# Attention and FFN block on one core: the second head's weights loaded and bounded in the preamble, the third head's loaded one head sooner

## The reference

```python
def attn(hidden_states, wq, wkv, wo):          # H=32, DN=DV=128, DQ=192
    q = (hidden_states @ wq).reshape(B, S, H, DQ)
    kv = hidden_states @ wkv                   # k: first H*DN columns, v: next H*DV
    scores = einsum('bqhd,bkhd->bhqk', q[..., :DN], k) * DQ ** (-0.5)
    probs = softmax(where(causal, scores, -1e30), axis=-1)
    attn = einsum('bhqk,bkhd->bqhd', probs, v).reshape(B, S, H * DV)
    return attn @ wo
x = x + attn(layernorm(x), wq, wkv, wo)
x = x + ffn(layernorm(x), k0, s0, k1, s1, k2, s2)
```

## Time and profile before

| | us |
|---|---|
| median of 3 runs (lowest, highest) | 1177.06 (1173.53, 1177.54) |
| the profiled execution's own time | 1173.75 |
| its span | 1171.9 |
| PE busy | 1092.5 (93%) |
| DVE busy | 895.7 (76%) |
| ACT busy | 677.0 (58%) |
| POOL busy | 677.7 (58%) |
| start of head 1's first scores on PE | 91.61 |

### The profile page before, as it was taken

One profiled execution on the slowest core, in us unless ns is written; L12 is line 12 of the kernel. 1 busy time (PEld: TensorE's weight loads), 2 busy tenths in 40 slices (PEclk: granted clock), 3 DMA queues, 4 the chain that ended last, 5 costly groups with the idle time before them and its releaser, 6 DMA issues. The chain is left out here.

```text
span 1171.9 us, 22406 instructions
## 1 busy us (share of the span) xinstructions
PE 1092.5 (93%) x6216; PEld 655.7 (56%) x6216; DVE 895.7 (76%) x1799; ACT 677.0 (58%) x1335; POOL 677.7 (58%) x694
## 2 busy tenths in 40 slices
PE   4658999999999999999999999999999999999898
PEld 3424555656556565656555565656555565655577
DVE  6556778787878787887878787887877787886873
ACT  5446565656566565656566556656566556655453
POOL 2406766656666766656666756656666756655400
PEclk9878999999999999999999999999999999999999
DMA  3126574646554474645554474545654474644601
GB/s 125 28 70 112 99 125 85 126 102 125 98 113 87 98 128 83 123 104 125 101 115 82 101 130 83 122 103 123 107 112 76 102 130 83 117 91 83 118 1 72
DMA packets 367800, 117.41 MB, mean 100 GB/s; under 512 B 313248, under 2 KB 361632, under 8 KB 367776
## 3 DMA queue, kind: packets, MB, share of 16 engines
q1 hardware_dynamic: 367776, 117.12, 50.9%
HBM read 39.45 MB, written 2.12 MB: 35 GB/s over the span
## 5 line engine op out<-in xcount | busy, mean ns | idle before, releaser
L1113 PE MATMUL psC<-xb,wqk 128*128 128x512 f16 x1350 | 323.7, 383 | 6.4 <-ACT x L671 4.1
L978 DVE CUSTOM_DVE_ANT_0 psS<-psS,mask,undo_qk 128x128 f32<-128x128 f32 (+7 forms) x256 | 210.9, 824 | 117.3 <-PE psS L1113 103.7
L549 POOL TENSOR_TENSOR qkT<-qk,qkT 128x512 f16<-128x512 f32 x124 | 143.1, 1159 | 246.5 <-ACT qkT L712 246.5
L1113 PE MATMUL psC<-wos,attn 128*128 128x512 f32 x768 | 249.7, 435 | 28.5 <-DVE attn L968 26.8
L719 ACT ACTIVATE psS<-psS,negmax 128x128 f32<-128x128 f32 (+7 forms) x256 | 182.6, 713 | 136.4 <-DVE negmax L978 134.2
L1113 PE MATMUL psS<-qkT 128*128 128x512 f16 (+3 forms) x1152 | 232.5, 330 | 24.4 <-DVE p L985 12.0
L985 DVE SCALAR_TENSOR_TENSOR p<-psS,p 128x128 f16<-128x128 f32 (+7 forms) x256 | 192.6, 753 | 42.3 <-ACT p L727 40.8
L1113 PEld LDWEIGHTS psC<-xb,wqk 128*128 128x128 f16 x1350 | 123.9, 98 | 162.2 <-issue 34.0
L1231 PE MATMUL psC<-pT,v 128*128 128x512 f16 (+3 forms) x1152 | 199.5, 328 | 0.8 <-DMA pT<-p 0.6
L1001 DVE SCALAR_TENSOR_TENSOR res<-psC,rinv,res 128x512 f32<-128x512 f32 x256 | 189.3, 744 | 6.9 <-DVE rinv L992 3.3
L1113 PE MATMUL psC<-wvs,xb 128*128 128x256 f16 x1536 | 190.5, 275 | 0.0
(11 more groups left out here) (90 smaller groups left out, 925.4 us busy)
## 6 DMA issues: line engine op xcount, KB each, us to landing
raw<-in_L_attn_wkv SPq DMA_DIRECT2D x64, 256.0 KB, 3.5
raw<-in_L_attn_wq SPq DMA_DIRECT2D x32, 256.0 KB, 3.5
raw<-in_L_attn_wo SPq DMA_DIRECT2D x32, 256.0 KB, 4.0
pT<-p SPq DMA_TRANSPOSE x256, 4.3
wrow<-wmax_rows SPq DMA_DIRECT2D x46, 64.0 KB, 3.4
res<-in_L_attn_hidden_states SPq DMA_DIRECT2D x8, 256.0 KB, 5.7
out<-res SPq DMA_DIRECT2D x8, 256.0 KB, 2.0
raw<-in_L_ffn_k SPq DMA_DIRECT2D x3, 256.0 KB, 4.5
```

The lines of the kernel that those rows point to most:

```text
L549: nc.gpsimd.tensor_tensor(lo, qk32[:, AT[n], :], hi, ALU.subtract) \
L978: nc.vector.tensor_tensor_reduce(row, row, mask[:, S - width:S], undo_qk[:, j % 2:j % 2 + 1], 3e38, ALU.add, ALU.min, negmax[:, n:n + 1]). ...
L1113: last = nc.tensor.matmul(out_ap, w, x, start=k == 0, stop=k == len(terms) - 1)
```

## The change

1. Head 1's query and key weights are loaded in the preamble, ahead of input tiles 4 to 7. ACT sums their squares in the preamble (`mx0@3` ahead of the `keep` steps), PE spreads them with a third transpose, and DVE makes the scale right behind that of the values. The trip through DRAM (`put0@3 get0@3`) is gone. The scaling (`r0@3`) moves ahead of the first plain product's copy.
2. Head 2's weights are loaded in the front and not in group 0. Their squares come behind `h3` of head 0, the `put` and `get` stand between `t0` and `t1` of head 0, and the scale comes behind `m7` of head 0.
3. The order of the front is another: scores and value projections of head 0 alternate, sums of inputs and their parts stand elsewhere, and steps up to `s7`, `m7`, `h7` now belong to the front's string. Input difference `T3` gets a block of its own (`B12` keeps the old one), so it no longer waits for the plain products and values; two differences live in another part of `pT`, and `t0` of head 1 waits for their low parts.
4. Waits that other waits already cover are dropped: `put` no longer waits for the previous `get`, nor `get` for the previous bound; `squares` gets one slot for each user and waits for the previous squares only.
5. The steady SP string is rotated: `put1 t0 t1 lo0 get1` of the next pair stood at its end and now stand at its start.

```diff
-B11, B21, T3, B22, T1, T2, T4 = range(7)
+B11, B21, B12, B22, T1, T2, T3, T4 = range(8)
...
 TENSOR_ORDERS
-    y0@2 y1@2 turn4@2 turn5@2 turn6@2 turn7@2 v0@2 v1@2 v2@2 s0@2 v3@2 y2@2 s1@2 y3@2 s2@2 v4@2 s3@2 v5@2 s4@2 v6@2
-    s5@2 v7@2 x1@3 s6@2 x2@3""", "")
+    spread2@2 y0@2 y1@2 turn4@2 turn5@2 turn6@2 turn7@2 v0@2 s0@2 v1@2 s1@2 v2@2 v3@2 y2@2 s2@2 y3@2 s3@2 x1@3 v4@2
+    s4@2 x2@3 v5@2 s5@2 x3@3 v6@2 s6@2 v7@2 s7@2""", "")
...
 SYNC_ORDERS
-    t2@-1 t3@-1 t4@-1 put0@1 t5@-1 t6@-1 lqk0@2 get0@1 t7@-1 t0@0 put0@2 t1@0 t2@0 t3@0 t4@0 lo0@0 get0@2 t5@0 lv0@2
-    t6@0 lqk0@3 t7@0 put1@2 t0@1 t1@1 lo0@1 get1@2""", """
-    lqk0@3 put0@3 get0@3 lo0@2 t0@2 t1@2 t2@2 t3@2""", "")
+    put1@0 t0@-1 t1@-1 lo0@-1 get1@0 t2@-1 t3@-1 t4@-1 put0@1 t5@-1 t6@-1 lqk0@2 get0@1 t7@-1 t0@0 put0@2 t1@0 t2@0
+    t3@0 t4@0 lo0@0 get0@2 t5@0 lv0@2 t6@0 lqk0@3 t7@0""", """
+    lqk0@4 lo0@2 t0@2 put0@4 get0@4 t1@2 t2@2 t3@2 t4@2""", "")
...
 def rows_to_dram(q, g, j, n):
-            if n:
-                wait_pair(q, rows_max[1], g, 1, j, 1)
-                q.sem_inc(queue_go, 1)
-                wait_pair(q, rows_in[1], g, 16, j, -16)
...
+            (wait_pair if n else wait)(q, rows_max[n], g, 1, j, 1)
...
 (preamble of SP)
             load_values(sp, 0)
+            load_head(sp, 1, 1)
             for t in range(4, NT):
...
 def row_squares(g, j, n):
                 at = 2 if n else j % 2
+                (wait_pair if n else wait)(act, rows_max[n], g, 1, j, 0 if n else -1)
...
-                    wait(act, rows_out[0], g, 16, j, -32)
                     src = raw[:, j % 2 * 2:j % 2 * 2 + 2, :]
-                nc.scalar.activation(squares[:, :], src.rearrange("p a s -> p (a s)"), ACT.Square,
+                nc.scalar.activation(squares[:, at, :], src.rearrange("p a s -> p (a s)"), ACT.Square,
...
 def bounds(g, j, n):
-                first = isinstance(g, int) and (GH * g + j == 0 or n and g + j // GH == 0)
-                if first:
-                    dve.wait_ge(spread_done, n + 1)
-                    rows = psC[:, 3, n * P:(n + 1) * P]
+                if isinstance(g, int) and (GH * g + j <= 1 or n and g + j // GH == 0):
+                    k = (0, 2)[GH * g + j] if n == 0 else 1
+                    dve.wait_ge(spread_done, k + 1)
+                    rows = psC[:, 3, k * P:(k + 1) * P]
...
+            def spread(k):
+                n, at, count = ((0, 0, 1), (1, 2, 1), (0, 1, 2))[k]
+                pe.wait_ge(rows_max[n], count)
+                if k == 2:
+                    pe.wait_ge(bounded[0], 1)
+                    pe.wait_ge(bounded[1], 1)
+                nc.tensor.transpose(psC[:, 3, k * P:(k + 1) * P], wmax[:, at:at + 1].to_broadcast([P, P]),
+                                    ident[:, :]).then_inc(spread_done, 1)
```

More of the change, by code:

```diff
@@ L50 @@
     h0@1 e1@1 h1@1 snap0@2 pv0@0 e2@1 h2@1 v6@0 v7@0 e3@1 h3@1 e4@1 h4@1 e5@1 h5@1 pv1@0 r1@2 e6@1 h6@1 qk0@2""", """
[L51 to L54, removed]
+    nhi0@2 nhi1@2 mx1@2 nhi2@2 nhi3@2 mx0@3 keep0@2 keep1@2 keep2@2 keep3@2 r1@2 root1@2 r0@3 y0@2 vhi0@2 vhi1@2
+    y1@2 nhi4@2 nhi5@2 nhi6@2 nhi7@2 keep4@2 keep5@2 keep6@2 keep7@2 v0@2 e0@2 h0@2 v1@2 e1@2 h1@2 v2@2 v3@2 y2@2
+    e2@2 h2@2 y3@2 part0@2 e3@2 h3@2 mx0@4 part1@2 snap0@3 v4@2 e4@2 h4@2 v5@2 e5@2 h5@2 part2@2 v6@2 part3@2 e6@2
+    h6@2 v7@2 r0@4 e7@2 h7@2""", "")
 VECTOR_ORDERS = ("""
@@ L258, in build @@
         wmax = sb("wmax", [P, 3], F32)
-        squares = sb("squares", [P, 2 * 512], F32)
+        squares = sb("squares", [P, 3, 2 * 512], F16)
         wrow = sb("wrow", [P, 3, P], F32)
@@ L265, in build @@
         w_all = sb("w_all", [P, 3, DC, D], F32R)
-        with nc.sbuf_tensor("xb", [P, 7, 2, 2, CH], F16) as xb, nc.sbuf_tensor("pT", [P, 2, BLOCKS, P], F16) as pT:
+        with nc.sbuf_tensor("xb", [P, 8, 2, 2, CH], F16) as xb, nc.sbuf_tensor("pT", [P, 2, BLOCKS, P], F16) as pT:
             pass
@@ L273, in build @@
                for t in (pT[:, 1, 32:64, :], pT[:, 1, 0:32, :])]
-        t32 = [t[:, :, :].rearrange("p (k c) s -> p k c s", c=2) for t in (xn, qk32)]
+        t32 = [xn[:, :, :].rearrange("p (k c) s -> p k c s", c=2),
+               pT[:, 1, 64:96, :].rearrange("p a s -> p (a s)").bitcast(F32).rearrange("p (k c s) -> p k c s", k=2, c=2)]
         X11, X21, X12, X22 = (x32[k // 2][:, k % 2] for k in range(4))
@@ L381, in build @@
         T_SUMS = ((XT3, X12, X22), (XT2, X11, XT3), (XT1, X12, X11), (XT4, X21, XT2))
-        T_PARTS = ((T2, XT2), (T1, XT1), (T4, XT4), (T3, XT3))
+        T_PARTS = ((T2, XT2), (T3, XT3), (T1, XT1), (T4, XT4))
         T_READY = {T2: 2, T1: 3, T3: 1, T4: 4}
@@ L418, in rows_from_dram @@
             at = 2 if n else j % 2
[L419 to L426, removed]
+            (wait_pair if n else wait)(q, rows_out[n], g, 16, j, 0 if n else -16)
             q.dma_start(wrow[:, at, :], wmax_dram[at, :].partition_broadcast(P)).then_inc(rows_in[n], 16)
@@ L898, in gather @@
                     wait(dve, x1_kept, g, 1, j, 0)
-                if isinstance(g, int) and GH * g + j == 1:
-                    dve.wait_ge(t_lo, T_USED[T1 if n < 4 else T4])
                 reused = {2: Q0, 3: Q1, 4: K0, 5: K1}.get(n)
@@ L1126, in norm_transpose @@
                 last.then_inc(xt_done, 1)
-            def spread(n):
-                pe.wait_ge(rows_max[n], 1)
-                nc.tensor.transpose(psC[:, 3, n * P:(n + 1) * P], wmax[:, 2 * n:2 * n + 1].to_broadcast([P, P]),
+            def spread(k):
[5 more added lines that the diff above has]
+                nc.tensor.transpose(psC[:, 3, k * P:(k + 1) * P], wmax[:, at:at + 1].to_broadcast([P, P]),
                                     ident[:, :]).then_inc(spread_done, 1)
@@ L1201, in project_v @@
                 if isinstance(g, int) and g + j // GH == 0:
+                    if n == 0:
+                        pe.wait_ge(bounded[0], 6)
                     if n % 4 == 0:
@@ L1208, in project_v @@
                 for d in range(DC):
-                    b = (B11, B21, T3, B22)[n // 4 * 2 + d // 2]
+                    b = (B11, B21, B12 if isinstance(g, int) and g + j // GH == 0 else T3, B22)[n // 4 * 2 + d // 2]
                     terms += halves(lambda w: xb[:, b, w, d % 2, n % 4 * P:(n % 4 + 1) * P], lambda w: wvs[:, w, d, :])
@@ L1245, in tensor_step @@
                     norm_transpose(n)
+                elif step == "spread":
+                    spread(n)
                 elif step == "s":
```

22 lines of the change are left out of this document (6 added, 16 removed).

## The result

| | before | after |
|---|---|---|
| median of the first comparison, 4 runs each (lowest, highest) | 1175.93 (1173.53, 1177.54) | 1165.38 (1164.79, 1165.53) |
| the pair again, in one later session (15 and 5 runs) | 1172.14 (1170.50, 1173.56) | 1165.43 (1163.94, 1167.35) |
| the profiled execution's own time | 1173.75 | 1165.53 |
| its span | 1171.9 | 1163.7 |
| head 1's first scores on PE (the marker) | 91.61 | 84.01 |

The ratio of the first comparison is 0.9911, with the interval 0.9891 to 0.9931; of the second 0.9941, 0.9928 to 0.9955. Faster by 0.9% and by 0.6%. After reads the same in both (1165.4). Before's four runs of the first comparison lay high: its medians in the three later sessions, each on another chip, are 1172.55 (21 runs), 1173.44 (11) and 1172.14 (15).

A forecast was written before the change was run, and what follows sets the result against it. PE bounds the loop but not the front, so gains lie before head 1's first scores. The walk gives 1173.75 less 4.6, 1169.15; with 1.75 for before's mean the forecast is 1170.9, range 1165 to 1176.

The forecast's parts named there:

- To the first score and y2: Front, PE: idle from 30.6 to 33.05, 1.8 added for a lower clock, y2 ends at 41.9.
- To m3: Front, head 0: m3 at 47.85, before 54.05; gain 6.2, all from the 8 us wait, less the idle PE.
- m3 to m5: Front, head 0's maxima: m4 at 53.7 (before 58.39), gain 4.7; m5 5.5 later at 59.2 (before 4.9 later).
- m6: Head 0's t1 on SP behind head 2's put and get; h5 waits 1.5 us (bounds 0, 6.0), m6 at 67.75.
- m7: Front, head 0: 6.45 behind m6 (before 6.12, now with v7's low part), at 74.2, before 74.86; gain down to 0.65.
- Behind m7: Front: the second wait goes, x7 takes 2.74 after idle time, a7 ends at 84.95, marker at 87.0, 4.6 us sooner.
- The base: Whole kernel: before's four known times have a mean of 1175.5, 1.75 over the profiled one; 1169.15 becomes 1170.9.
- Dropped waits, loop: Loop: dropped waits stand beside others that end later, and the SP string cut at another place changes nothing.
- A: Front, lighter chain: PE keeps its clock (1.8), h5's wait goes (1.5), x7 at full clock (1.3); 1167.6, all 1166.3; chance 0.28.
- B: Front, SP: trip takes 10.2, t1 lands after 7.6, 6.6 us more at h5, marker about unchanged; 1175.5; chance 0.12.
- C: Front: head 2's column comes too late, the 8 us wait stays behind m7, gain and wait cancel; 1177; chance 0.03.
- D: Loop's boundary on SP: late t0 makes h4 wait once per pass; a 5.7 us boundary costs 11, 1182; chance 0.05.

The follow-up runs named there:

- after_again: The changed kernel without an edit, measured beside before in one later session: median 1165.43 us, ratio to before 0.9941.
- head2_late: Changed kernel with head 2's weights loaded and squared late and its put and get around the fifth transpose, as before: 1166.80 us, ratio to before 0.9952.
- queue_moved: Changed kernel with head 2's put on SP moved behind head 0's third transpose and its get behind the fourth: 1164.03 us, ratio to before 0.9920.
- queue_gather: queue_moved with head 1's gather a4 ahead of the low part of tile 7 on DVE: 1162.12 us, ratio to before 0.9905.
- head1_dram_early: Changed kernel with head 1's column through DRAM, not the third transpose on PE, its squares still in the preamble: 1165.08 us, ratio to before 0.9928.
- head1_dram_late: Changed kernel with part 1 undone: head 1's weights squared as late as before and its column through DRAM again: 1169.45 us, ratio to before 0.9974.
- all_moves: Changed kernel with the edits of queue_gather and v1_first together: 1160.27 us, ratio to before 0.9900.
- v1_first: Changed kernel with value chain v1 ahead of head 0's first scores on PE: 1163.87 us, ratio to before 0.9918.
- before_again: The kernel before without an edit, for a second profile: 1172.52 us, marker at 90.10.

## Why the prediction was wrong in its size

The direction, the places of the waits and the order of events were right; the gain came out too small. The forecast was 1170.9, the median is 1165.4, at the lower edge of the range given. The 5.5 us between them have three parts: the walk (3.0), the time that before was measured from (1.75), and what lies behind the marker (0.6); the rest, 0.15, is between the profiled execution and the median. Of the walk's own signs of being wrong one came true: m3 was at 44.69 and not near 48. The marker also lies outside its 85 to 91.

**The walk, 87.0 forecast, 84.01 profiled.**
- *To the first score and y2: the failed step.* y2 ends at 38.34, not 41.9. Of the 3.6 us, 1.8 is the term "After an idle time of 2.42 a value chain took 2.76 ... I take that row and add 1.8", which wasn't paid: the idle time was 1.84, and after 1.83 or 1.84 us the chain took its full-clock 1.47 in all five profiles that have it (after, `after_again`, `head2_late`, `queue_moved`, `queue_gather`). Another 0.9 is the term "everything of tiles 4 to 7 is 0.9 late", which didn't reach PE. DVE did start the statistics of these tiles later (6.96 us behind the first transposes, before 6.12), but its four normalisations took 2.76 us where they took 3.71 in before, and from the first transposes on PE to the end of the last there are 14.69 us, before 14.78. Why they were quicker isn't shown. The last 0.97 is no effect of the change: the first transposes start at 12.79, at 13.76 in before's profile, and in `after_again` at 14.46. Counted from the first transposes, y2 ends after 25.6 and 25.7 us in the two profiles of after, where the forecast has 28.1. The term of the clock isn't imaginary: `head1_dram_early` paid 1.67 after 2.40 us. But I had put it in whole, from a single row of a single execution.
- *To m3: the size near, the reason too narrow.* "All of it from the 8 us wait" doesn't hold. DVE's first wait for `wrow` was 5.57 us (the 8.1 of the earlier trace rows is the second), and by `head1_dram_late` some 4.5 of the 9.4 us come from part 1 and 3.9 from the rest of the change, the rest being the start.
- *m3 to m5: right.* From m3 to m4 6.0 us, forecast 5.85; from m4 to m5 5.48, forecast 5.5. The 3 us lead of y2 stays.
- *m6: right in kind, too small.* h5 waited 2.88 for `t1`, forecast 1.5, with its place and cause as written. The trip took 7.7, not 8.1; but h5 came 5.0 after the issue of `t1` at 56.16, where I had a landing of 3.1. `queue_moved` shows the price: 1.4 in the medians, 2.6 in the marker of one profile. By an estimate from the fixed 2 us of the Trainium skill (DMA: Bandwidth & Descriptors, Anatomy of one DMA; that section goes by the gpsimd path, and here SP issues) h5 would not have waited. It did: the trips of 512 bytes took 7.7 in after and 7.7 and 8.1 in `head1_dram_late` and `head1_dram_early`, so the traces do not agree with that figure here.
- *m7: right.* 6.46, forecast 6.45.
- *Behind m7: right, but for x7.* The bound waits for nothing, ACT scales at 74.05 ahead of e7 at 75.11. x7 took 1.47, where I had 2.74 for the half clock (1.3). The idle time of over 4 us was there, but ahead of x5 and x6, which took the half clock (5.30 us for the two); ahead of x7 it was 1.91. Other executions had 1.85 to 2.74 for x7. From a7's end at 82.01 to the marker 2.0, as forecast.

The marker of one program moved by 1.9 us between two profiles, so a part of the walk's 3.0 is the luck of the profiled execution. Its own time, 1165.53, is close to the median, that of `after_again`, 1167.35, is not.

**The base.** I added 1.75 us because before's known times lay above the profiled one in the mean. The 47 later runs have medians of 1172.1 to 1173.4, all three below the profiled 1173.75. It fitted before's median of the first comparison (1175.93), but not after, whose profiled 1165.53 is close to its medians. Four times with a spread of 4 us were too few to correct a profile by; without the correction the forecast would have been 1169.15.

**"Dropped waits, loop: nothing".** That step failed by a little: 1.5 us in the medians, some of it behind the marker. That a wait is covered by a later one says that it holds nobody up, not that the engine passes it for free; this is my reading, not shown.

**The rivals.** A was nearest: of its three parts the kept clock (over 1.84 us of idle time, not 2.4) and x7's full clock came (3.1 us), and the h5 wait did not go. B (SP eats it) had the right place, but 2.9 us and not 8. C and D are out: the second column was there in time, and no cost of the loop's boundary on SP shows. Behind the marker the kernel takes 1079.7, before 1080.3, and of the two runs on before the one with the ring turned takes 1079.1, the other 1079.6.

**What the change was made of.** Part 1 gives 4.1, part 2 1.4 (2.8 if the queue is ordered for it), the dropped waits about 1.5; together 7.0, with 6.7 measured in one session (7.2 and 8.0 across sessions). The two DVE waits that went summed to 13.6 us, and 7.6 of it arrived at the marker. The rest went to work that moved into head 0's chain (the distance from m3 to m5 grew by 2.3 us against before) and to the wait of h5 behind the DMA pair (m5 to m6 grew by 3.9). With three more moves in the order, `all_moves` has its marker 12.7 us before that of the earlier trace rows. Part 3 wasn't undone by itself. The sum leaves next to nothing for it, and `head1_dram_late` shows its lead at m3 and none at m7; what it gives on its own stays open.

## What to carry to other kernels

A wait that is removed pays only up to the next thing that is late, so walk to the first point that the bound engine sees and sum up there. A dependent pair of DMAs in a strict queue holds everything behind it for its whole trip (7 to 9 us here), and before that for as long as its first half waits for its input (12.9 us here): issue what is already ready ahead of it or between its halves. Prices that come and go between executions (a dropped clock, a late start) belong into the range with a chance, not into the sum in full.

## What the runs showed of the hardware that was not expected

- The granted clock is not decided by the program alone. The same chain after the same idle time of 2.5 us took 1.46 us in one execution and 2.30 in another (granted clock 1.00 and 0.61); two kernels with 2.40 and 2.49 us of idle time before the first score got 2.25 and 1.47 for the value chain behind it (0.62 and 1.00).
- The quicker x5 and x6, the slower x7. In six profiles x7 starts 7.2 us behind x5. Where x5 and x6 took 5.30 us, x7 came after 1.91 us of idle time and took 1.47 (after, `head1_dram_late`); with 5.09 it was 2.11 and 1.85 (`v1_first`), with 4.97 2.24 and 2.09 (`queue_moved`), with 4.82 2.39 and 2.39 (`after_again`), with 4.33 2.88 and 2.74 (`head1_dram_early`). The shorter the two took, the later x7 ended, from 8.7 to 9.9 us behind x5's start.
- The trip of a 512-byte column to DRAM, from the issue of the write to that of the read behind it, took in these fronts from 6.9 us (`before_again`, 72.25 to 79.14) to 8.6 (`head2_late`, 67.18 to 75.80), in both with a transpose issued between. Little of it is moving data: in after all 144 packets of the write lie between 48.5 and 49.2, at most 1.2 us behind its issue, and from there to the issue of the read at 55.72 the DMA engines show one packet, of an instruction queue.
- The first transposes on PE start between 12.79 and 14.46 us in four profiles of the two kernels, which shifts all that follows by as much.
